# Graph message passing on one Trainium2 core: 20 chunks of edges move from gathering to counting, and the message add moves from VectorE to GpSimd

## The chip, the cores and the metric

The kernel runs on one core of one Trainium2 chip. A core has five engines that run their own instruction streams in order and meet through semaphores: TensorE (PE), VectorE (DVE), ScalarE (ACT), GpSimd (POOL) and SyncE (SP, which here only issues DMAs). The metric is the device time of one launch in microseconds. The kernel before was timed at 1654.11 us, the median of 3 runs (1650.71 to 1654.78).

## The reference

12,500 nodes have 64 features each; 400,000 edges, sorted by destination, have 64 features each. Most edges end at low node numbers, because the destination is drawn as 12,500 times the square of a uniform number.

```python
src = randint(400000, 0, 12500)
dst = (12500 * uniform(400000) ** 2).astype(int32)        # then both are sorted by dst
msg = node_feat[src] + edge_feat
agg = segment_sum(msg, dst, num_segments=12500)
h   = relu(agg @ W1 + b1)                                  # 64 -> 128
out = layernorm(x + h @ W2 + b2, axis=-1)                  # 128 -> 64, eps 1e-5
```

## The kernel before

**Chunks.** The edges are cut into 625 chunks of 640 (128 partitions by 5 columns). Every chunk has a *job*: SP loads the chunk's edge features, DVE compares the edges' destinations with 64 consecutive node numbers and writes a 0/1 matrix (`mark`, L809), PE multiplies five 128x64 blocks of features by it (`product`, L1026), and DVE adds the 64x64 result into the aggregate `agg` in SBUF (`add`, L831). Two jobs share a PSUM bank, and `add` runs two jobs behind `mark` (LAG = 2), so that DVE waits for both products of the pair.

**Two ways to get x[src].** The jobs above sum only edge features. The part with `x[src]` is brought in differently for the two kinds of chunk. For the last 205 chunks (the *gathered* ones, nodes of high number) POOL fetches the rows `x[src]` by indirect DMA, five instructions of 128 rows per chunk (`gather`, L550), into one of five slots of `xmsg`, and DVE adds them to the edge features before the product (`mix`, L803). For the first 420 chunks (the *counted* ones: CROWS = 84 rows of 5 chunks) nothing is gathered: the kernel counts how often each source node occurs for each destination node, and multiplies these counts by x.

**Counting.** Windows of 1 to 4 consecutive nodes get *passes* of 128 edges. Up to ten passes make a *slot*. For each slot DVE compares the low 7 bits of the sources (`oh_lo`, L847) and the high part together with the node (`oh_key`, L851) with row constants; PE multiplies the two (`count_slot`, L1042) and so counts in PSUM; ACT copies the counts of a unit of 3 to 5 nodes into `counts` (`keep_unit`, L652). About 128 nodes make a *block*, and for each block PE multiplies the counts of 98 groups of 128 source nodes by x, split into three bf16 parts (`multiply`, L1058: 98 matmuls per block, spread over the next block's slots). The sums are turned (L1070) and added to `agg`. Every 128 passes make a *group*, for which DVE searches the place of the edges in a table (L763, L768), POOL fetches the records (`load_records`, L559), DVE prepares keys (L776, L778), PE turns them (L1004, L1005) and ACT copies them (L628).

**What sets the order.** The order on every engine is written out ahead of time by slot number. `plan` makes units, slots and groups from the expected edge counts. `timeline` gives each slot a planned time between FIRST and LAST, by its cost, and deals out the gathers and the jobs: the gather number g stands before the slot whose planned time reaches 36 + chunk x g/5. All engines go through the slots 0, 1, 2, ... and put the jobs that belong to the slot ahead of its counting. Rings of three (`oh_lo`, `oh_key`, PSUM banks) keep DVE at most three slots ahead of PE. On SP, the load of a chunk into a slot of `gmsg` or `cmsg` waits for the product that used the slot before.

After the loop, 13 batches of nodes go through the two dense layers and the normalization (L1125 to L1139, L591).

Of the kernel before, what the change touches and what calls it, by code (L numbers as in the profile page):

```python
# [9 lines left out]
LN_EPS = 1e-5  # L10
PARTS = 3
TOP = 256
CROWS = 84
FINE = 16
RARE = 1e-7

# [81 lines left out]
def timeline(units, slots, groups, gathered, counted):  # L98

    cost = [x.n * (195 + 92 * x.width) + 500 for x in slots]  # L100
    S, total = len(slots), sum(cost)
    FIRST, LAST = 90.0, 36.0 + 6.8 * gathered + 1.4 * groups
    begin, run = [], 0
    for c in cost:
        begin.append(FIRST + (LAST - FIRST) * run / total)
        run += c
    chunk = (LAST - 36.0) / gathered
    gathers_at = [[] for _ in range(S + 1)]
    s = 0
    for g in range(5 * gathered):  # L110
        while s < S and begin[s] < 36.0 + chunk * g / 5:
            s += 1
        gathers_at[s].append(divmod(g, 5))
    jobs = [(36.0 + chunk * (k + 1) + 5.0, "gather", k) for k in range(gathered)]
    jobs += [(70.0 + (LAST - 70.0) * (i + .5) / counted, "count", i) for i in range(counted)]
    jobs.sort()
    jobs_at = [[] for _ in range(S + 1)]
    s = 0
    for place, (_, kind, i) in enumerate(jobs):
        t = jobs[min(place | 1, len(jobs) - 1)][0]  # L120
        while s < S and begin[s] < t:
            s += 1
        jobs_at[s].append((place, kind, i))
    return gathers_at, jobs_at


def build(nc, x, src, dst, edge_attr, w1, b1, w2, b2, out):
    f32, i32, i16, bf16 = mybir.dt.float32, mybir.dt.int32, mybir.dt.int16, mybir.dt.bfloat16
    f16 = mybir.dt.float16
    ALU, ACT, AX = mybir.AluOpType, mybir.ActivationFunctionType, mybir.AxisListType  # L130

    N, D = x.shape
    E = src.shape[0]
    HID = w1.shape[1]
    TILES = 5
# [4 lines left out]
    RT = TILES * TILES  # L140
    CCH = CROWS * TILES
    GCH = NCH - CCH
# [13 lines left out]
    LAST = N - (HI - 1) * P  # L156
# [3 lines left out]
    FINES = ROW // FINE  # L160
    CFINE = CROWS * FINES
    UNITS, SLOTS, WINDOWS, RANGES = plan(N, E, COUNTED, HI)
# [32 lines left out]
    for b in range(BLOCKS):  # L195
# [4 lines left out]
        to = min(s0 + n + 2, NS)  # L200
# [8 lines left out]
    OSLOTS = 4  # L209
    RING = 3  # L210
    TABLES = 3
    GSLOTS, XSLOTS, CSLOTS = 8, 5, 6

    edge_v = edge_attr.rearrange("(c p j) f -> c p (j f)", p=P, j=TILES)
    src_v = src.rearrange("(t e) -> t e", t=ROWS)
# [8 lines left out]
    with ExitStack() as ctx:  # L224
        def sb(name, shape, dt=f32):
            return ctx.enter_context(nc.sbuf_tensor(name, shape, dt))

        def sem(name):
            return ctx.enter_context(nc.semaphore(name))
# [18 lines left out]
        gmsg = sb("gmsg", [P, GSLOTS * TILES * D])  # L248
        xmsg = sb("xmsg", [P, XSLOTS * TILES * D])
# [38 lines left out]
        src_f, hi_i = stage[:, 0:ROW], stage[:, ROW:2 * ROW].bitcast(i32)  # L288
        record_out = counts[0][0:CROWS, 0:FINES * REC].bitcast(f32).rearrange("t (b k) -> t b k", k=REC // 2)
        pad_out = onehot[0][:, 0:5 * REC // 2]  # L290
# [56 lines left out]
        gin = [sem(f"gin{s}") for s in range(GSLOTS)]  # L347
        gathered = [sem(f"gathered{s}") for s in range(XSLOTS)]
        mixed = sem("mixed")
# [43 lines left out]
        for r, (b, w, j) in enumerate(WINDOWS):  # L393
            if j == 0:
                t = 1
# [10 lines left out]
        def _(sp):  # L406
# [32 lines left out]
            for i in range(CSLOTS):  # L439
                load_counted(i)  # L440

            sp.wait_ge(most_made, 1)
            sp.dma_start(most_dram.rearrange("(t k) -> t k", t=CROWS), most[0:CROWS, :]).then_inc(most_out, 16)
            sp.wait_ge(records_made, 2)
            sp.dma_start(record_dram[0:CFINE, :].rearrange("(t b) k -> t (b k)", t=CROWS),
                         counts[0][0:CROWS, 0:FINES * REC].bitcast(i16)).then_inc(records_out, 16)
            sp.wait_ge(most_out, 16)
# [64 lines left out]
        def _(pool):  # L512
# [32 lines left out]
            def gather(k, j):  # L545
                t = k % XSLOTS
                if k >= XSLOTS and j == 0:
                    pool.wait_ge(mixed, k - XSLOTS + 1)
                at, of = t * TILES + j, k * TILES + j
                pool.indirect_dma_start(xmsg[:, at * D:(at + 1) * D], None, x,  # L550
                                        bass.IndirectOffsetOnAxis(ap=idx_t[:, of:of + 1], axis=0)
                                        ).then_inc(gathered[t], 16)

            def load_records(g):
                pool.wait_ge(run_ready, g + 1)
                pool.wait_ge(records_out, 32)
                if g >= 2:
                    pool.wait_ge(tables_turned, g - 1)
                pool.indirect_dma_start(records[g % 2][:, :], None, record_dram,  # L559
                                        bass.IndirectOffsetOnAxis(ap=run_at[g % 2][:, 0:1], axis=0)  # L560
                                        ).then_inc(records_in[g % 2], 16)

            pool.wait_ge(taken["idx"], NTURNS["idx"])
            for s in range(NS + 1):
                for g in SEARCH.get(s - 3, []):
                    load_records(g)
                for k, j in GATHERS_AT[s]:
                    gather(k, j)
                    if (k, j) == (2, 4):
                        for g in range(EARLY_GROUPS):  # L570
                            load_records(g)

            pool.wait_ge(redo_known, 1)
            redo = pool.value_load(redo_i[0:1, 0:1], min_val=0, max_val=1)
# [145 lines left out]
        def _(dve):  # L720
# [74 lines left out]
            nc.vector.tensor_copy(node_ps, iota_row[:, :]).then_inc(iotas_set, 1)  # L795
            dve.wait_ge(iotas_set, 3)

            def mix(k):
                s, t = k % GSLOTS, k % XSLOTS
                dve.wait_ge(gin[s], 16 * (k // GSLOTS + 1))  # L800
                dve.wait_ge(gathered[t], 16 * TILES * (k // XSLOTS + 1))
                to = gmsg[:, s * TILES * D:(s + 1) * TILES * D]
                nc.vector.tensor_tensor(to, to, xmsg[:, t * TILES * D:(t + 1) * TILES * D], ALU.add).then_inc(mixed, 1)  # L803

            def mark(place, kind, i):
                c = i if kind == "count" else CCH + i
                if place >= OSLOTS:
# [54 lines left out]
            for s in range(NS + 1):  # L862
                for place, kind, i in JOBS_AT[s]:
                    mark(place, kind, i)
                    if kind == "gather":
                        mix(i)
                    if place >= LAG:
                        add(place - LAG)
                if s == NS:
                    for place in range(NCH - LAG, NCH):  # L870
                        add(place)
                for g in SEARCH.get(s, []):
                    search(g)
                for g in SUBTRACT.get(s, []):
                    subtract(g)
                for b in ADD_SUMS.get(s, []):
                    add_sums(b)
                if s in (3, 7):
                    k = s // 4
                    for h in range(2):  # L880
                        take_part(h, k)
                    dve.wait_ge(b2_parted, k + 1)
                    nc.vector.tensor_tensor(b2_sb[:, :], b2_sb[:, :], b2_parts[:, k, :], ALU.subtract).then_inc(b2_rest, 1)
                if s < NS:
                    make_slot(s)
# [20 lines left out]
            with dve.If(0 < redo):  # L906
# [5 lines left out]
                with dve.Fori(0, NCH) as c:  # L912
# [4 lines left out]
                    with dve.Fori(0, extra + 1) as w:  # L917
# [8 lines left out]
                        to = agg[:, bass.ds((first_at + w * WIN).with_bounds(min_val=0, max_val=N - 1), WIN)]  # L926
# [250 lines left out]
```

## Time and profile before

| | |
|---|---|
| median of 3 runs | 1654.11 us |
| the profiled execution | 1654.78 us, its span 1652.9 us |
| TensorE busy | 1415.9 us (86% of the span), granted clock 0.915 of full speed |
| VectorE busy | 1374.4 us (83%) |
| GpSimd busy | 1085.5 us (66%) |
| ScalarE busy | 841.5 us (51%) |
| gathers (L550) | 1025 instructions, 980 ns each |
| counting matmuls (L1042) | 4206 |
| matmuls of counts by x (L1058) | 4410, that is 45 blocks of 98 |

The profiled execution is one of the timed runs; the span goes from its first to its last instruction. Busy time is the union of an engine's instructions. The first 100 us are the set-up (sorting out the lists, the first gathers), the loop over the slots runs from about 101 to 1519 us, and the dense layers take the rest. In PE's and DVE's busy times by line, the end of an instruction overlaps the start of the next, so the lines of an engine add up to more than its union.

### The profile page before, as it was taken

How to read it: one execution, taken by the hardware profiler on the slowest of the kernel's cores; microseconds unless marked ns; L12 is line 12 of the kernel's file. 1: busy time of each engine (PE TensorE's matmuls, PEld its weight loads, DVE VectorE, ACT ScalarE, POOL GpSimd, SP SyncE). 2: the span in 40 equal slices, each digit the busy share in tenths (PEclk: the TensorE clock that was granted, in tenths of full speed). 3: DMA queues.
4: the chain of work that ended last, by engine and by line, in shares of the span. 5: the costliest groups of instructions: out<-in, count | busy, mean ns of one | idle time of the engine just before them, and what ended most of it. 6: DMA issues, size and time to landing. Idle time of an engine off the chain costs nothing.

```text
span 1652.9 us, 43132 instructions
## 1 busy us (share of the span) xinstructions
PE 1415.9 (86%) x15541; PEld 1181.1 (71%) x15542; DVE 1374.4 (83%) x3536; ACT 841.5 (51%) x1767; POOL 1085.5 (66%) x1138
## 2 busy tenths in 40 slices
PE   1155788888898988989999989999999999999996
PEld 1155666667787877867766668888888888888454
DVE  4479999989998998989989989888888888885233
ACT  1233446575355565554444445566566666664332
POOL 9677777777777776767667776666657676653011
PEclk8577889999999999999999999999999999999555
DMA  3733444444444443434443443333334333331122
GB/s 105 183 93 92 118 105 113 101 105 109 110 107 106 115 115 95 111 100 98 114 101 98 104 106 95 92 99 99 93 100 102 91 95 97 94 88 27 40 56 60
DMA packets 159195, 162.47 MB, mean 98 GB/s; under 512 B 53803, under 2 KB 141723, under 8 KB 158653
## 3 DMA queue, kind: packets, MB, share of 16 engines
q1 hardware_dynamic: 124603, 122.83, 26.2%
q0 software_dynamic: 34384, 36.90, 12.3%
q8 instruction: 126, 2.06, 0.5%
q14 instruction: 82, 0.67, 0.1%
HBM read 154.75 MB, written 4.85 MB: 97 GB/s over the span
## 4 chain that ended last, share of the span: by engine, by line
PE 46%; DVE 31%; issue 15%; DVEq 3%; POOL 2%; ACT 2%; DMA 1%; SPq 0%; POOLq 0%
PE sums_ps L1058 14%; DVE oh_key L851 13%; PE counted_ps L1042 12%; PE chunk_ps L1026 11%; DVE oh_lo L847 6%; DVE onehot L809 4%; PE counted_ps L1125 3%; PE chunk_ps L1139 3%; DVE lists L831 2%; POOL counts L520 2%; DVE gmsg L803 2%; PE turn_ps L1070 2%; DVE less_b L763 1%; DVEq L823 1%; PE chunk_ps L1135 1%
## 5 line engine op out<-in xcount | busy, mean ns | idle before, releaser
L550 POOL DMA_INDIRECT xmsg<-in_x,idx_t x1025 | 1004.5, 980 | 321.9 <-issue 309.4
L652 ACT CAST counts<-counted_ps 128x392 bf16<-128x392 f32 (+2 forms) x1375 | 675.2, 545 | 584.8 <-PE counted_ps L1042 570.6
L1042 PE MATMUL counted_ps<-oh_key,oh_lo 128*128 128x196 bf16 (+3 forms) x4206 | 513.2, 251 | 103.2 <-DVE oh_key L851 89.6
L851 DVE TENSOR_TENSOR oh_key<-counted_ps,tables 128x980 bf16<-128x980 f16 (+4 forms) x883 | 537.3, 608 | 0.0
L1058 PE MATMUL sums_ps<-x_parts,counts 128*128 128x193 bf16 (+4 forms) x4410 | 497.7, 250 | 0.0
L1058 PEld LDWEIGHTS sums_ps<-x_parts,counts 128*128 128x128 bf16 (+4 forms) x4410 | 399.0, 110 | 39.0 <-issue 2.1
L1042 PEld LDWEIGHTS counted_ps<-oh_key,oh_lo 128*128 128x128 bf16 x4206 | 289.9, 100 | 187.8 <-DVE oh_key L851 127.6
L847 DVE TENSOR_TENSOR oh_lo<-counted_ps,tables 128x640 bf16<-128x640 f16 (+3 forms) x883 | 406.0, 460 | 15.5 <-PE counted_ps L1042 14.1
L1026 PE MATMUL chunk_ps<-onehot,cmsg 128*64 128x64 f32 x4200 | 315.4, 228 | 12.0 <-DVE lists L831 12.0
L1026 PEld LDWEIGHTS chunk_ps<-onehot,cmsg 128*64 128x64 f32 x4200 | 277.0, 141 | 44.8 <-issue 37.5
L809 DVE TENSOR_TENSOR onehot<-counted_ps,rel_t 128x320 f32<-128x320 f32 x625 | 296.9, 475 | 0.4 <-issue 0.3
L831 DVE TENSOR_TENSOR lists<-lists,chunk_ps 64x64 f32 x625 | 128.4, 205 | 120.1 <-PE chunk_ps L1026 77.1
L1026 PE MATMUL chunk_ps<-onehot,gmsg 128*64 128x64 f32 x2050 | 166.6, 232 | 6.5 <-DVE gmsg L803 5.9
L1026 PEld LDWEIGHTS chunk_ps<-onehot,gmsg 128*64 128x64 f32 x2050 | 142.6, 144 | 24.6 <-DVE gmsg L803 12.1
L559 POOL DMA_INDIRECT records<-edge_records,run_at x33 | 31.3, 949 | 109.8 <-DVE run_at L768 106.2
L803 DVE TENSOR_TENSOR gmsg<-gmsg,xmsg 128x320 f32<-128x320 f32 x205 | 97.2, 474 | 0.0
L591 POOL TENSOR_TENSOR x_parts<-x_parts,rstd 128x512 f32<-128x512 f32 (+1 forms) x13 | 12.9, 993 | 127.2 <-DVE rstd L951 127.2
L937 DVE TENSOR_TENSOR x_parts<-chunk_ps,x_parts 128x512 f32<-128x512 f32 (+1 forms) x13 | 8.6, 661 | 72.8 <-PE chunk_ps L1139 71.6
L656 ACT ACTIVATE counted_ps<-counted_ps,less_top 128x392 f32<-128x392 f32 (+2 forms) x100 | 55.5, 555 | 3.2
L1139 PEld LDWEIGHTS chunk_ps<-w_sb,x_parts 128*128 128x128 f32 x196 | 42.8, 330 | 10.2 <-issue 10.2
L1125 PE MATMUL counted_ps<-lists,w_sb 64*128 (+2 forms) x50 | 46.2, 1079 | 1.8 <-issue 1.8
L1139 PE MATMUL chunk_ps<-w_sb,x_parts 128*128 128x64 f32 x196 | 45.2, 425 | 0.0
(94 smaller groups left out, 479.6 us busy)
## 6 DMA issues: line engine op xcount, KB each, us to landing
cmsg<-in_edge_attr SPq DMA_DIRECT2D x420, 160.0 KB
gmsg<-in_edge_attr SPq DMA_DIRECT2D x205, 160.0 KB
xmsg<-in_x,idx_t POOLq DMA_INDIRECT x1025
x_parts<-in_x SPq DMA_DIRECT2D x12, 256.0 KB, 3.3
out_nodes<-x_parts SPq DMA_DIRECT2D x12, 256.0 KB, 2.6
edge_records<-counts SPq DMA_DIRECT2D x1, 1575.0 KB
lists<-in_src SPq DMA_DIRECT2D x1, 1562.5 KB
lists<-in_dst SPq DMA_DIRECT2D x1, 1562.5 KB
```

The lines of the kernel that those rows point to most:

```text
L550: pool.indirect_dma_start(xmsg[:, at * D:(at + 1) * D], None, x, bass.IndirectOffsetOnAxis(ap=idx_t[:, of:of + 1], axis=0)).then_inc(gathe ...
L652: nc.scalar.copy(to, ps.rearrange("p (n h) -> p h n", h=HI)).then_inc(unit_kept, 1)
L803: nc.vector.tensor_tensor(to, to, xmsg[:, t * TILES * D:(t + 1) * TILES * D], ALU.add).then_inc(mixed, 1)
L809: nc.vector.tensor_tensor(onehot[place % OSLOTS][:, :].rearrange("p (j n) -> p j n", j=TILES), node_ps.unsqueeze(1).broadcast_to([P, TILES ...
L831: nc.vector.tensor_tensor(to, to, chunk_ps[place // 2 % 2][0:D, place % 2 * WIN:place % 2 * WIN + w], ALU.add).then_inc(added, 1)
L847: nc.vector.tensor_tensor(oh_lo[s % RING][:, 0:n * P].rearrange("p (k n o) -> p k n o", k=n, o=2), lo_ps.rearrange("p (n o) -> p n o", o=2 ...
L851: nc.vector.tensor_tensor(oh_key[s % RING][:, 0:n * w].rearrange("p (k n o) -> p k n o", k=n, o=2), key_ps[:, 0:w].rearrange("p (n o) -> p ...
L1026: mm = nc.tensor.matmul(chunk_ps[place // 2 % 2][0:D, place % 2 * WIN:place % 2 * WIN + w], rows_at[:, j * D:(j + 1) * D], onehot[place % ...
L1042: mm = nc.tensor.matmul(unit_ps[u % BANKS][:, col:col + slot.key_cols], oh_lo[s % RING][:, n * P:(n + 1) * P], oh_key[s % RING][:, n * slo ...
L1058: mm = nc.tensor.matmul(sums_ps[0:n, 0:XC], counts[b % 2][:, h * P:h * P + n], x_parts[:, h * XC:(h + 1) * XC], start=(h == 0), stop=(h == ...
L1125: mm = nc.tensor.matmul(count_ps[k][:, o:o + m], w1_sb[:, :], agg[:, bass.ds(within(b * FN + o, AGG - m), m)], start=True, stop=True)
L1139: mm = nc.tensor.matmul(chunk_ps[k][:, i * D:(i + 1) * D], hid[k][:, i * P:(i + 1) * P], w2_sb[:, :], start=False, stop=(i == n - 1), skip ...
```

## The change

CROWS goes from 84 to 88, so 440 chunks are counted and 185 gathered, where it was 420 and 205. By `plan` this gives 940 slots instead of 883, 4482 passes instead of 4206, 1513 units instead of 1375, 50 blocks instead of 45 and 36 groups instead of 33. The first 4206 passes are nearly the same; what is new is the counting for nodes 5716 to 6267 at the end.

`mix` moves from DVE to POOL, behind the second gather of the next chunk. `gmsg` gets ten slots instead of eight and `xmsg` three instead of five. The constants of `timeline` change: LAST becomes 36 + 7.4 x 185 + 1.4 x 36 (1455.4) where it was 36 + 6.8 x 205 + 1.4 x 33 (1476.2), and a gathered chunk's job stands 0.4 of a chunk and 1 us later after its gathers.

```diff
-CROWS = 84
+CROWS = 88
@@ timeline
-    FIRST, LAST = 90.0, 36.0 + 6.8 * gathered + 1.4 * groups
+    FIRST, LAST = 90.0, 36.0 + 7.4 * gathered + 1.4 * groups
...
-    jobs = [(36.0 + chunk * (k + 1) + 5.0, "gather", k) for k in range(gathered)]
+    jobs = [(36.0 + chunk * (k + 1.4) + 6.0, "gather", k) for k in range(gathered)]
@@ build
-    GSLOTS, XSLOTS, CSLOTS = 8, 5, 6
+    GSLOTS, XSLOTS, CSLOTS = 10, 3, 6
@@ gpsimd
+            def mix(k):
+                s, t = k % GSLOTS, k % XSLOTS
+                pool.wait_ge(gin[s], 16 * (k // GSLOTS + 1))
+                pool.wait_ge(gathered[t], 16 * TILES * (k // XSLOTS + 1))
+                to = gmsg[:, s * TILES * D:(s + 1) * TILES * D]
+                nc.gpsimd.tensor_tensor(to, to, xmsg[:, t * TILES * D:(t + 1) * TILES * D], ALU.add).then_inc(mixed, 1)
...
                 for k, j in GATHERS_AT[s]:
                     gather(k, j)
+                    if j == 1 and k:
+                        mix(k - 1)
...
+            mix(GCH - 1)
@@ vector
-            def mix(k):
-                s, t = k % GSLOTS, k % XSLOTS
-                dve.wait_ge(gin[s], 16 * (k // GSLOTS + 1))
-                dve.wait_ge(gathered[t], 16 * TILES * (k // XSLOTS + 1))
-                to = gmsg[:, s * TILES * D:(s + 1) * TILES * D]
-                nc.vector.tensor_tensor(to, to, xmsg[:, t * TILES * D:(t + 1) * TILES * D], ALU.add).then_inc(mixed, 1)
...
                 for place, kind, i in JOBS_AT[s]:
                     mark(place, kind, i)
-                    if kind == "gather":
-                        mix(i)
                     if place >= LAG:
                         add(place - LAG)
```

POOL, from its first gather on, before (`xmsg` are the gathered rows, `records` the fetched groups):

```order
L550 DMA xmsg<-in_x,idx_t 128x64 x15
L559 DMA records<-edge_records,run_at 128x384 x2
L550 DMA xmsg<-in_x,idx_t 128x64 x57
L559 DMA records<-edge_records,run_at 128x384
L550 DMA xmsg<-in_x,idx_t 128x64 x21
```

The same place after (L559 is now the line of `mix`, L566 that of the records):

```order
L550 DMA xmsg<-in_x,idx_t 128x64 x7
L559 TENSOR_TENSOR gmsg<-gmsg,xmsg 128x320
L550 DMA xmsg<-in_x,idx_t 128x64 x5
L559 TENSOR_TENSOR gmsg<-gmsg,xmsg 128x320
L550 DMA xmsg<-in_x,idx_t 128x64 x3
L566 DMA records<-edge_records,run_at 128x384 x2
L550 DMA xmsg<-in_x,idx_t 128x64 x2
L559 TENSOR_TENSOR gmsg<-gmsg,xmsg 128x320
```

After each five gathers POOL now carries one add of 128x320, with two gathers of the next chunk between a chunk's last gather and its add.

DVE in the late part of the loop before, a pair of jobs between two slots (`onehot` is `mark`, `lists` holds `agg`, the ISA rows set the address of the add):

```order
L851 TENSOR_TENSOR oh_key0<-counted_ps,tables0 128x980
L809 TENSOR_TENSOR onehot2<-counted_ps,rel_t 128x320
L803 TENSOR_TENSOR gmsg<-gmsg,xmsg 128x320
L831 ISA
L831 TENSOR_TENSOR lists<-lists,chunk_ps0 64x64
L809 TENSOR_TENSOR onehot3<-counted_ps,rel_t 128x320
L831 ISA
L831 TENSOR_TENSOR lists<-lists,chunk_ps0 64x64
L847 TENSOR_TENSOR oh_lo1<-counted_ps,tables0 128x640
```

And after, a like pair:

```order
L854 TENSOR_TENSOR oh_key0<-counted_ps,tables2 128x980
L812 TENSOR_TENSOR onehot2<-counted_ps,rel_t 128x320
L834 ISA
L834 TENSOR_TENSOR lists<-lists,chunk_ps0 64x64
L812 TENSOR_TENSOR onehot3<-counted_ps,rel_t 128x320
L834 ISA
L834 TENSOR_TENSOR lists<-lists,chunk_ps0 64x64
L850 TENSOR_TENSOR oh_lo1<-counted_ps,tables1 128x640
```

Only the add of `gmsg` and `xmsg` is gone from DVE; the rest stands as it did.

PE in the added slots at the end of the loop after (L1043 counts, L1059 multiplies counts by x, L1027 are the products of the jobs):

```order
L1043 MATMUL counted_ps<-oh_key0,oh_lo0 128x196 x5
L1059 MATMUL sums_ps<-x_parts,counts1 128x193 x10
L1043 MATMUL counted_ps<-oh_key1,oh_lo1 128x196 x5
L1059 MATMUL sums_ps<-x_parts,counts1 128x193 x10
L1027 MATMUL chunk_ps1<-onehot2,cmsg 64x64 x5
L1027 MATMUL chunk_ps1<-onehot3,gmsg 64x64 x5
```

A slot of five passes carries about nine or ten matmuls of counts by x, as in the last third of the loop before.

## Rows read from the trace of the kernel before

**Rows 1.** The page: busy time, then 40 slices and granted clock.
```profile
PE 1415.9 (86%) x15541; PEld 1181.1 (71%) x15542; DVE 1374.4 (83%) x3536; ACT 841.5 (51%) x1767; POOL 1085.5 (66%) x1138
...
PE   1155788888898988989999989999999999999996
...
DVE  4479999989998998989989989888888888885233
```

**Rows 2.** Busy by stretch: window, length, PE, PEld, DVE, ACT, POOL, clock, DMA, GB/s.
```profile
101.30:278.00 176.70, 124.88 (x1523) 106.10 (x1523) 167.94 (x380) 75.00 (x149) 137.38 (x130) 0.85 0.41 104
278.00:674.00 396.00, 350.22 (x4406) 304.02 (x4403) 369.94 (x924) 228.53 (x461) 292.22 (x303) 0.97 0.43 107
674.00:1049.20 375.20, 343.52 (x3634) 269.82 (x3634) 343.32 (x1045) 184.27 (x382) 260.18 (x271) 0.99 0.41 103
1049.20:1516.00 466.80, 451.89 (x5372) 407.22 (x5373) 403.74 (x1047) 288.49 (x703) 305.99 (x318) 0.99 0.36 92
```

**Rows 3.** Waits, 101.3 to 278 us: total, times, longest.
```profile
PE counted_ps L1042 <- DVE oh_key L851: 43.7, 39, 7.5
```

**Rows 4.** Waits from 1049.2 to 1516 us.
```profile
POOL records L559 <- DVE run_at L768: 65.7, 10, 9.8
DVE lists L831 <- PE chunk_ps L1026: 37.9, 36, 3.3
...
PE counted_ps L1042 <- DVE oh_key L851: 7.7, 8, 2.8
```

**Rows 5.** Timeline, DVE around one mix: start, duration, line.
```profile
178.43 0.20 DVE L831 TENSOR_TENSOR lists<-lists,chunk_ps 64x64 f32 x1
178.56 0.48 DVE L809 TENSOR_TENSOR onehot<-counted_ps,rel_t 128x320 f32<-128x320 f32 x1
178.96 0.47 DVE L803 TENSOR_TENSOR gmsg<-gmsg,xmsg 128x320 f32<-128x320 f32 x1
179.36 0.21 DVE L831 TENSOR_TENSOR lists<-lists,chunk_ps 64x64 f32 x1
```

**Rows 6.** PE by line, 1049.2 to 1516 us: L1042, then L1058, then L1026.
```profile
1049.20:1516.00 466.80, 161.58 (x1305) 0.99 0.36 92
...
1049.20:1516.00 466.80, 207.88 (x2027) 0.99 0.36 92
...
1049.20:1516.00 466.80, 131.25 (x1900) 0.99 0.36 92
```

**Rows 7.** Timeline, DVE, a slot without a job.
```profile
1304.94 0.48 DVE L847 TENSOR_TENSOR oh_lo<-counted_ps,tables 128x640 bf16<-128x640 f16 x1
...
1305.35 0.65 DVE L851 TENSOR_TENSOR oh_key<-counted_ps,tables 128x980 bf16<-128x980 f16 x1
...
1305.92 0.47 DVE L847 TENSOR_TENSOR oh_lo<-counted_ps,tables 128x640 bf16<-128x640 f16 x1
```

**Rows 8.** POOL's groups by shape: count, busy, mean ns, idle before.
```profile
L550 POOL DMA_INDIRECT xmsg<-in_x,idx_t x1025 | 1004.5, 980 | 321.9 <-issue 309.4 <-DVE gmsg L803 11.5 <-PE turn_ps L1005 0.6
...
L591 POOL TENSOR_TENSOR x_parts<-x_parts,rstd 128x512 f32<-128x512 f32 x12 | 12.5, 1043 | 127.2 <-DVE rstd L951 127.2
L520 POOL IOTA counts<- 1x1426 int16 x2 | 12.1, 6052 | 0.0
...
L591 POOL TENSOR_TENSOR x_parts<-x_parts,rstd 128x128 f32<-128x128 f32 x1 | 0.4, 401 | 0.0
```

**Rows 9.** Timeline, POOL and DVE: first gather, and one beside L860.
```profile
39.70 1.13 POOL L550 DMA_INDIRECT xmsg<-in_x,idx_t  x1 [0.16 <-issue]
...
104.56 0.95 POOL L550 DMA_INDIRECT xmsg<-in_x,idx_t  x1 [0.30 <-issue]
...
105.81 7.67 POOL L550 DMA_INDIRECT xmsg<-in_x,idx_t  x1 [0.30 <-issue]
105.92 6.74 DVE L860 TENSOR_TENSOR counts<-counts,x_parts 128x3136 f32<-128x3136 f32 x2
```

**Rows 10.** Timeline, POOL: the fifth gather of the chunk mixed at 178.96.
```profile
174.56 1.09 POOL L550 DMA_INDIRECT xmsg<-in_x,idx_t  x1 [0.30 <-issue]
```

## The prediction

> **What bounds the kernel now.** I read first the page's busy shares and slices. PE (86%) and DVE (83%) are both near the top, and their digits change places: DVE has the nines in the first half, PE in the second [rows 1]. An average can't decide here, so I cut the loop into four stretches [rows 2]. Their ends are the starts of the slots 88, 308, 616 and 882, found by counting the `oh_key` instructions, so that jobs and mixes can be counted for each. From 101 to 278 us DVE is busy 95% and PE 71%, and PE waits for `oh_key` [rows 3]: DVE bounds. From 278 to 674 it is DVE 93%, PE 88%; from 674 to 1049 both 91.5%. From 1049 to 1516 PE is busy 97% and DVE 86%; there DVE waits for PE's products (37.9 us) and PE hardly for DVE (7.7 us) [rows 4]. So PE bounds the last third, DVE the first eighth, and between them the two take turns, with 7 to 9% lost to their short rings. Last I looked at POOL, which takes the new work. Its gathers run back to back, and its idle time is a wait for DVE's search before the records, 65.7 us in the last third alone [rows 4]. It is ahead there and has room.
>
> **The parts of the change.** The order is fixed by slot number, so I cost the old slots and the added ones apart. All durations are from the profiled execution: 1654.8 us, a span of 1652.9 us and 1.9 us around it; the median is 0.7 us lower.
>
> *The mix leaves DVE.* By its record it lasts 0.47 us, but records overlap: it starts at 178.96 and the next instruction at 179.36, so it takes 0.40 us of DVE's time [rows 5]. The four stretches hold 25, 57, 54 and 62 mixes: 10.0, 22.8, 21.6 and 24.8 us.
>
> *Jobs are thinned out.* The same 625 jobs spread over 940 slots. By `timeline` the four stretches lose 4, 10, 12 and 12 jobs to the end and two go from slot 0, 40 in all. On DVE a job is a mark and an add, 0.40 and 0.13 us [rows 5]. On PE its ten records take 131.3/190 = 0.69 us; but PE's lines add up to more than the union (523 to 451.9 us in the last stretch, the small lines among them), so I count 0.863 of it, 0.60 us [rows 2, 6].
>
> *The old slots.* Now each stretch is as long as its longer engine allows. How full that engine gets I take from the stretches themselves: 95% for DVE a third ahead, 97% for PE 12% ahead, 91.5% where both are equal [rows 2].
> First: DVE 167.9 - 10.0 - 2.1 = 155.8, at 95% 164.0 us, 12.7 saved.
> Second: DVE 369.9 - 22.8 - 5.3 = 341.8; PE 350.2 - 6.0 = 344.2. They are equal now; at 92% that is 374 us, 22 saved, not the 28 by which DVE was relieved.
> Third: DVE 343.3 - 21.6 - 6.4 = 315.3; PE 343.5 - 7.2 = 336.3. PE is ahead by 6%; at 94.3%, between the two cases, 356.6 us, 18.6 saved.
> Fourth: DVE 403.7 - 24.8 - 6.4 = 372.5; PE 451.9 - 7.2 = 444.7, now 19% ahead; at 97.5% 456.1 us, 10.7 saved.
> Together 64 us. DVE is relieved of nearly 100 us, and the rest is covered by PE.
>
> *The added slots.* 57 slots, with 276 passes of the 196-column form, 490 matmuls for 5 blocks, the 40 jobs, 5 turns and 3 tables. On PE, each from the last stretch [rows 6]: 276 x 161.6/1305 = 34.2; 490 x 207.9/2027 = 50.3; 40 x 0.69 = 27.6; turns and tables some 6. The sum is 118, by 0.863 102, at 97.5% 104 us. A check: the last 267 slots before took 466.8 us, 1.75 us each, and 57 such are 100 us, in spite of slightly fewer products of counts in each. DVE needs 57 x 0.98 us [rows 7], 40 x 0.53 and a few us for three groups, 83 us, so it is not late; ACT copies 138 more units in the shade of both. Nothing hides these 104 us: they stand behind a PE that is already full.
>
> *POOL.* A gather takes 0.98 us and 0.30 us of issue in the mean; undisturbed, 0.94 and 0.30, 1.25 us from start to start [rows 8, 9]. 925 of them are 1156 us. The mix is not shown on POOL. The nearest row is the multiply of the last phase: 1043 ns for 512 columns, 401 for 128 [rows 8]; for 320 columns that gives 722 ns, and with the issue gap 1.02 us. From below it can't cost less than the 0.40 us of DVE; from above I take the 1.04 us of 512 columns, the gap, and a wait for the gathers to land. This wait is not shown either. A mix on DVE started 3.3 us after its fifth gather ended without having waited [rows 5, 10]; two gathers now cover about 2.5 us, so it is between nothing and 0.8 us. So a mix is 0.4 to 2.1 us; I take 1.02, the row. POOL then needs 1156 + 189 + 36 x 1.25 = 1390 us from 43 us on and would be done at 1433, over 100 us before the loop ends; that is the cover. It is thinnest early: by the order, POOL must have issued 322 gathers by slot 264, which is 43 + 402 + 66 + 10 = 521 us, where PE and DVE arrive at about 545. The wait for the records now stands ahead of mixes too; but the order puts a mix some 5 slots before its product, and POOL's wait ends as DVE's search does, before PE is there: nothing.
> The two engines can also block each other. The gather beside L860 took 7.67 us where its neighbours took 0.95, until DVE's add of two SBUF operands was done [rows 9]. If every add on POOL held DVE up like that, it would cost 185 x 0.72 = 133 us of DVE. Against it, gathers take their 0.95 us beside DVE's steady stream of adds and compares with one operand in PSUM, and those are nearly all of the loop: I take nothing, and put the other end under D.
> The Trainium skill has the rule between these two ends (SBUF — State Buffer, Who interferes with whom): the engines share a port pair as a lock, and an instruction of VectorE takes part in it when both its inputs are in SBUF or in a two-port mode. By the rule the loss is nothing but a few key copies; without it, up to 133 us of DVE.
> The Trainium skill speaks against the move (GPSIMD Engine Reference, 4.1 Engine selection): adds of two tensors belong on VectorE, GpSimd being some 2x slower. Row and rule agree, 0.72 against 0.40 to 0.47 us. By the rule the move loses where POOL bounds; by the rows POOL doesn't, and the sum is the same.
>
> *Start.* POOL's lists are 276 and 108 entries longer, in two copies; at 6052/1426 = 4.2 ns each [rows 8] that is 3.2 us, and the set-up waits for them; two more loads stand on SP, about 1 us. Two jobs and the mixes fewer in slot 0 give some 2 us back: +2 us. The bounds are 0 and 5 us.
>
> Sum: 1654.8 - 64 + 104 + 2 = 1696.8; less 0.7 for the median, 1696 us, 2.5% slower.
>
> **The rivals.**
> *A: DVE bounds the whole loop (faster).* For it: PE's busy is a model, and DVE has more nines early. If the loop went by DVE alone at its 90.8%, its work would go from 1284.9 us by -79 (mixes) -20 (jobs) +83 to 1269: (1269 - 1284.9)/0.908 = -17 us, with the start 1639 us. The place is the added slots: PE would have to take their 102 us into gaps. It decides by how full PE can be from 278 us on: its 1350 us of work less the first stretch's 122 are 1228; at 98% the kernel is as fast as before, and A needs 99.6%. Against it: from 1049 us on DVE waits for PE. 5%.
> *B: PE and DVE mesh better.* With slack on DVE the middle stretches fill as the last, all at 97.5%: 160 + 353 + 345 + 456 = 1314 for 1414.7, a gain of 101: 1660 us. For it: the losses there are waits of one for the other. Against: equal loads made these losses. 7%.
> *C: POOL becomes the bound.* It begins early when a mix with gap and wait is over about 1.4 us, and at the end when over 1.7. At 2.0 us POOL ends at 43 + 1156 + 45 + 370 = 1614, where the loop would have ended at some 1559: 1751 us. For it: the unknown landing and the small early slack. 10%.
> *D: the relief gives little.* Early gaps belong to the ring and stay; half the 64 us: 1728 us; none: 1760, and no less if POOL's adds block DVE. 8%.
> *My forecast* 70%, its own range 1675 to 1718.
>
> **How the numbers follow.** Changes within 0.3% (5 us) can't be told from none. Faster has A: 5%. The same has half of B: 4%. Slower has the rest, 91%. The range leaves out A and the far side of C and D: 1665 to 1735.
>
> **What would show it.** Loop end near 1560 us, not 1519. PE's busy total near 1500, at 97% in the last third; DVE's near 1355, at 91, 88 and 82% in the second to fourth stretch. L559 as TENSOR_TENSOR on POOL, 0.7 us, 185 times, with no wait above 1 us on the gathers; gathers at 0.95 us. Slot 616 at some 998 us where it was 1049. The forecast is wrong if PE waits for POOL's mix by over 20 us in total, if PE's records of the old slots get shorter, or if the first 883 slots take other than 1345 to 1360 us.

## The result: 3.2% slower, and the profile after

The changed kernel took 1706.98 us, the median of 3 runs (1704.24 to 1709.12), against 1654.11. The ratio is 1.0319 (95% interval 1.0302 to 1.0337). The forecast was 1696 us. The profiled span is 1703.1 us, 50.2 us more than before. The changed kernel ran twenty times in all, with a median of 1705.2 us; where an experiment differs from it by a few us only, I compare with that.

First the page of the kernel after: busy time, and PE and DVE in 40 slices.

```profile
PE 1472.2 (86%) x16343; PEld 1241.7 (73%) x16344; DVE 1356.6 (80%) x3465; ACT 901.4 (53%) x1918; POOL 1136.8 (67%) x1226
...
PE   1156788989899898999999899999999989999997
...
DVE  4469999999998888899899878887878877885233
```

PE gained 56 us and DVE lost 18 [rows 1]. DVE's nines are now rare after the first third. That alone doesn't say where the 50 us are, so I cut the loop at the same slots as before (0, 88, 308, 616, 882) and add the new slots and the end. The view gives window, length, then PE, PEld, DVE, ACT, POOL.

```profile
108.06:270.09 162.03, 117.41 (x1485) 99.31 (x1484) 155.51 (x347) 75.15 (x148) 128.31 (x125) 0.88 0.39 104
270.09:643.01 372.92, 335.68 (x4305) 293.82 (x4303) 342.90 (x847) 227.90 (x461) 287.77 (x308) 0.98 0.41 106
643.01:996.97 353.96, 327.70 (x3485) 263.90 (x3485) 316.44 (x967) 182.79 (x380) 255.42 (x275) 0.99 0.38 99
996.97:1462.33 465.36, 444.95 (x5266) 399.13 (x5265) 375.81 (x965) 288.03 (x702) 304.83 (x326) 0.99 0.34 90
1462.33:1558.95 96.62, 94.13 (x1121) 84.19 (x1119) 78.81 (x206) 62.86 (x154) 62.36 (x68) 1.00 0.28 69
1558.95:1703.00 144.05, 128.88 (x546) 81.85 (x544) 40.56 (x85) 39.78 (x58) 13.26 (x14) 0.60 0.20 45
```

Beside [rows 2] this is the whole account. The slots 0 and 882 of before stood at 101.3 and 1515.9 us.

| part | before | after | difference | forecast |
|---|---|---|---|---|
| set-up, until slot 0 | 101.3 | 108.1 | +6.8 | +2 |
| slots 0 to 88 | 176.8 | 162.0 | -14.8 | -12.7 |
| 88 to 308 | 395.9 | 372.9 | -23.0 | -22 |
| 308 to 616 | 375.3 | 354.0 | -21.3 | -18.6 |
| 616 to 882 | 466.7 | 465.4 | -1.3 | -10.7 |
| 57 new slots | - | 96.6 | +96.6 | } +104 |
| from the last slot to the end | 137.0 | 144.1 | +7.1 | } |

In the new slots PE is busy 97% and DVE 82%, and they are the loss. The +7.1 us of the end has a visible cause, in the timeline of PE after the last slot:

```profile
1560.95 8.55 PE L1059 MATMUL sums_ps<-x_parts,counts 128*128 128x193 bf16 x98
...
1573.46 8.55 PE L1059 MATMUL sums_ps<-x_parts,counts 128*24 128x193 bf16 x98
```

Before, one block of 98 matmuls stood alone at the end. Now there are two, since the 50th block has only 24 nodes and leaves the 49th hardly a slot to spread over; and a block of 24 nodes costs the 8.55 us of one of 128.

POOL kept up with its new work. First its add (shortest, median and longest in ns), its own waits for the gathers to land and the wait of PE's weight load for the add; then who waited for whom after, with total, times and longest:

```profile
L559 POOL TENSOR_TENSOR gmsg<-gmsg,xmsg x185: 856/872/887, 52.0 to 1558.5; 128x320 f32<-128x320 f32 x185
...
  DMA xmsg<-in_x,idx_t: 21.7, 21
...
  PEld chunk_ps L1027: 0.5, 3
```

```profile
POOL records L566 <- DVE run_at L778: 145.5, 24, 12.8
DVE lists L834 <- PE chunk_ps L1027: 124.7, 84, 10.4
...
DVE less_b L773 <- DMA most_b<-fine_most: 21.1, 1, 21.1
```

PE waited 0.5 us in all for POOL's adds, and POOL 21.7 us for gathers to land. POOL still waits for DVE's search, DVE waits more for PE's products than before (124.7 us to 77.1), and in the set-up DVE waits 21.1 us for the table, where it had been 11.4.

### The profile page after: what moved, and what is told of

Read it like the earlier page. It is cut to its first block, busy times and chain, and to the rows that moved or that the text cites. A ratio compares the mean times of both kernels' runs of the same rounds, so it can differ in the third digit from the quotient of the medians.

```text
span 1703.1 us, 45021 instructions
## 1 busy us (share of the span) xinstructions
PE 1472.2 (86%) x16343; PEld 1241.7 (73%) x16344; DVE 1356.6 (80%) x3465; ACT 901.4 (53%) x1918; POOL 1136.8 (67%) x1226
## 3 DMA queue, kind: packets, MB, share of 16 engines
q0 software_dynamic: 31328, 33.91, 10.6%
## 4 chain that ended last, share of the span: by engine, by line
PE 59%; DVE 20%; issue 12%; ACT 3%; POOL 2%; DVEq 2%; DMA 1%; SPq 1%; POOLq 0%
PE sums_ps L1059 19%; PE counted_ps L1043 16%; PE chunk_ps L1027 15%; DVE oh_key L854 8%; DVE oh_lo L850 5%; DVE onehot L812 3%; PE counted_ps L1126 3%; PE chunk_ps L1140 3%; POOL counts L520 2%; ACT counts L662 2%; PE turn_ps L1071 2%; DVE lists L834 2%; DVE less_b L773 1%; DVEq L826 1%; PE chunk_ps L1136 1%
## 5 line engine op out<-in xcount | busy, mean ns | idle before, releaser
L550 POOL DMA_INDIRECT xmsg<-in_x,idx_t x925 | 889.1, 961 | 257.3 <-issue 238.2
L662 ACT CAST counts<-counted_ps 128x392 bf16<-128x392 f32 (+2 forms) x1513 | 732.0, 540 | 566.8 <-PE counted_ps L1043 549.8
L1043 PE MATMUL counted_ps<-oh_key,oh_lo 128*128 128x196 bf16 (+3 forms) x4482 | 546.4, 250 | 98.6 <-DVE oh_key L854 80.3
L854 DVE TENSOR_TENSOR oh_key<-counted_ps,tables 128x980 bf16<-128x980 f16 (+4 forms) x940 | 570.6, 607 | 0.0
L1059 PE MATMUL sums_ps<-x_parts,counts 128*128 128x193 bf16 (+4 forms) x4900 | 545.6, 250 | 0.1
L1059 PEld LDWEIGHTS sums_ps<-x_parts,counts 128*128 128x128 bf16 (+4 forms) x4900 | 440.1, 107 | 39.4 <-issue 2.6
L850 DVE TENSOR_TENSOR oh_lo<-counted_ps,tables 128x640 bf16<-128x640 f16 (+5 forms) x940 | 430.1, 458 | 27.3 <-PE counted_ps L1043 25.1
L1043 PEld LDWEIGHTS counted_ps<-oh_key,oh_lo 128*128 128x128 bf16 x4482 | 315.1, 99 | 182.8 <-DVE oh_key L854 115.0
L1027 PE MATMUL chunk_ps<-onehot,cmsg 128*64 128x64 f32 x4400 | 326.0, 227 | 12.6 <-DVE lists L834 11.8
L1027 PEld LDWEIGHTS chunk_ps<-onehot,cmsg 128*64 128x64 f32 x4400 | 287.2, 141 | 46.0 <-issue 38.5
L834 DVE TENSOR_TENSOR lists<-lists,chunk_ps 64x64 f32 x625 | 126.1, 202 | 170.1 <-PE chunk_ps L1027 124.7
L559 POOL TENSOR_TENSOR gmsg<-gmsg,xmsg 128x320 f32<-128x320 f32 x185 | 161.5, 873 | 24.6 <-DMA xmsg<-in_x,idx_t 21.7
L1027 PE MATMUL chunk_ps<-onehot,gmsg 128*64 128x64 f32 x1850 | 147.5, 229 | 1.8 <-DVE lists L834 1.8
L1027 PEld LDWEIGHTS chunk_ps<-onehot,gmsg 128*64 128x64 f32 x1850 | 127.1, 143 | 16.1 <-issue 12.7
L566 POOL DMA_INDIRECT records<-edge_records,run_at x36 | 34.1, 946 | 150.9 <-DVE run_at L778 145.5
L773 DVE TENSOR_SCALAR_CACHE_REDUCE less_b<-most_b,node_t 128x777 bf16<-128x777 int16 (+33 forms) x36 | 32.0, 889 | 21.1 <-DMA most_b<-fine_most 21.1
```

The lines of the kernel that those rows point to most:

```text
L559: nc.gpsimd.tensor_tensor(to, to, xmsg[:, t * TILES * D:(t + 1) * TILES * D], ALU.add).then_inc(mixed, 1)
L662: nc.scalar.copy(to, ps.rearrange("p (n h) -> p h n", h=HI)).then_inc(unit_kept, 1)
L834: nc.vector.tensor_tensor(to, to, chunk_ps[place // 2 % 2][0:D, place % 2 * WIN:place % 2 * WIN + w], ALU.add).then_inc(added, 1)
L850: nc.vector.tensor_tensor(oh_lo[s % RING][:, 0:n * P].rearrange("p (k n o) -> p k n o", k=n, o=2), lo_ps.rearrange("p (n o) -> p n o", o=2 ...
L854: nc.vector.tensor_tensor(oh_key[s % RING][:, 0:n * w].rearrange("p (k n o) -> p k n o", k=n, o=2), key_ps[:, 0:w].rearrange("p (n o) -> p ...
L1027: mm = nc.tensor.matmul(chunk_ps[place // 2 % 2][0:D, place % 2 * WIN:place % 2 * WIN + w], rows_at[:, j * D:(j + 1) * D], onehot[place % ...
```

## Experiments

Every ratio is to the kernel before, on the same chip, with its 95% interval. Stretches are the slots' as above. My theory: the relief of DVE pays only where DVE bounds, and added slots stand behind PE. Its rivals are those of the prediction, above all A (DVE bounds throughout) and C (POOL becomes the bound).

### e1: CROWS = 88 alone

```diff
-CROWS = 84
+CROWS = 88
```

> The kernel before with CROWS = 88 and nothing else changed: the mix stays on VectorE (185 of them), eight and five slots, the old constants of the timeline. My theory (TensorE bounds the end of the loop, and the 57 added slots stand behind it in full): +104 us for the added slots and their end, +5 to +7 us in the set-up, about -20 us because 40 jobs and 32 mixes leave the first 883 slots; 1735 to 1755 us, ratio 1.05 to 1.06. Theory A (VectorE bounds throughout): its work rises by 83 - 20 - 8 = 55 us, 1715 us. A theory in which fewer gathers relieve the kernel: under 1690 us.

1740.05 us, ratio 1.0507 (1.0478 to 1.0536). The set-up is 8.4 us longer, the four stretches changed by -3.9, -0.8, -19.1 and +0.6 us, the new slots took 97.0 and the end 143. The 38 jobs and 31 mixes that left the old slots saved 23 us, nearly all in the third stretch, and the new slots cost as much as in the change, though the mixes are on DVE here. So more counting is the loss, and A's 1715 us is refuted.

### e2: the mix on VectorE, but one column

```diff
-                to = gmsg[:, s * TILES * D:(s + 1) * TILES * D]
-                nc.vector.tensor_tensor(to, to, xmsg[:, t * TILES * D:(t + 1) * TILES * D], ALU.add).then_inc(mixed, 1)
+                to = gmsg[:, s * TILES * D:s * TILES * D + 1]
+                nc.vector.tensor_tensor(to, to, xmsg[:, t * TILES * D:t * TILES * D + 1], ALU.add).then_inc(mixed, 1)
```

> The kernel before with the mix still on VectorE and all its semaphores, but adding one column of 320, so the output lacks most of x[src] for the gathered chunks. VectorE loses about 0.33 us for each of 205 mixes, 68 us, and GpSimd gets nothing. My theory (TensorE covers most of the relief): 40 to 50 us saved, some 10, 15, 15 and 5 us in the four stretches; 1605 to 1615 us. Theory A (VectorE bounds throughout): 68/0.908 = 75 us saved, 1580 us. Theory D (gaps belong to the ring): 20 us or less saved, over 1630 us.

1624.08 us, ratio 0.9827 (0.9810 to 0.9843): 30 us saved, less than the 40 to 50 I expected and far from the 75 of A. The stretches, in the same view:

```profile
101.50:273.10 171.60, 117.95 (x1520) 101.42 (x1519) 159.88 (x381) 75.29 (x149) 132.63 (x128) 0.87 0.42 107
...
1017.90:1483.20 465.30, 451.35 (x5372) 406.78 (x5373) 384.57 (x1047) 288.46 (x703) 300.00 (x318) 0.99 0.37 92
```

They saved 5.2, 14.7, 11.7 and 1.4 us. In the last one DVE lost 19 us of work and the stretch 1.4; PE is at 97% there as before. e1 and e2 together save 56 us in the old slots and the change 60, so its gain is about as large as the two reliefs together. By stretches they don't add up: e1 and e2 give 9.1, 15.5, 30.8 and 0.8 us, the change 14.8, 23.0, 21.3 and 1.3. That the totals are near is in part chance.

### e3: the added blocks hardly multiplied

```diff
-                for h in range(h0, h1):
+                for h in [h for h in range(h0, h1) if b < 45 or h in (0, HI - 1)]:
...
-            nc.vector.tensor_scalar(signs_row[:, 0:1], sums_ps[0:1, 256:257], float(COUNTED), None,
-                                    ALU.not_equal).then_inc(redo_step, 1)
+            nc.vector.tensor_scalar(signs_row[:, 0:1], sums_ps[0:1, 256:257], -1.0, None,
+                                    ALU.is_lt).then_inc(redo_step, 1)
```

> The changed kernel, in which the five added blocks (45 to 49) are multiplied by x for 2 of their 98 groups of sources only, and the test on the sum of counts always passes; their nodes' sums are wrong. 480 matmuls are gone from TensorE and nothing from the other engines. My theory (TensorE bounds the added slots): 480 x 0.0885 us = 42 us less, of which 17 in the two runs of 98 at the very end; 1660 to 1670 us. If VectorE bounds there: only the 17 us at the end, 1690 us.

1680.25 us, ratio 1.0165 (1.0141 to 1.0190), 27 us less than the change. It lies between the two forecasts, and the stretches say why:

```profile
1461.60:1549.20 87.60, 77.52 (x832) 58.77 (x830) 79.47 (x205) 61.23 (x154) 61.74 (x67) 0.98 0.31 75
```

The end got 16 us shorter, as expected. But the new slots went only from 96.6 to 87.6 us although PE lost about 17 us of work in them. PE is busy 88% and DVE 91% then, and PE's waits there are 4.8 us for ACT's copies, 2.5 us for DVE's keys and 1.5 us for `oh_key`; which of them holds the slots isn't shown. So PE bounds the new slots, but the next limit stands only 9 us behind; cheaper multiplies alone would not have saved the change.

### e4: the mix on GpSimd with the old split

```diff
-CROWS = 88
+CROWS = 84
```

> The changed kernel with CROWS = 84: the mix on GpSimd and all else of the change, but the old split into 420 counted and 205 gathered chunks. TensorE and VectorE alone would be done 60 us earlier than before, about 1595 us. GpSimd needs 1025 x 1.25 + 205 x (0.87 + 0.30) + 33 x 1.25 = 1562 us from 40 us on, with some 20 us of waits for landing, so it ends at some 1620 us, where the loop of before ended at 1519. My theory, that GpSimd's room is used up by 0.87 us adds and that this is what the fewer gathers pay for: 1730 to 1760 us. If GpSimd is not the bound: 1595 to 1600 us.

1711.56 us, ratio 1.0353 (1.0335 to 1.0370): POOL is the bound, though by less than I had worked out. Here is its stream, then the waits of this run:

```profile
803.03 0.94 POOL L550 DMA_INDIRECT xmsg<-in_x,idx_t  x1 [0.30 <-issue]
804.00 0.87 POOL L559 TENSOR_TENSOR gmsg<-gmsg,xmsg 128x320 f32<-128x320 f32 x1
805.03 0.96 POOL L550 DMA_INDIRECT xmsg<-in_x,idx_t  x1 [0.16 <-issue]
```

```profile
PE turn_ps L1005 <- DVE keys L788: 72.5, 22, 6.3
...
DVE lows L786 <- DMA records<-edge_records,run_at: 48.3, 18, 5.4
...
PE chunk_ps L1027 <- POOL gmsg L559: 24.6, 14, 6.6
```

One gather follows another at 1.25 us, and at 2.0 us with an add between: the add costs 0.75 us there. Its record says 0.87; it begins 0.03 us after the gather ends, and the gap before the next gather is 0.16 us instead of 0.30. POOL waits only 5.0 us for the search in the whole loop, so it is full, and its lateness arrives by two ways: PE waits 24.6 us for mixes, and DVE 48.3 us for the records, which stand behind adds and gathers on POOL; PE then waits for DVE's keys. So in the changed kernel the fewer gathers are what makes room for the adds. That POOL is the bound is read from these waits; no run took the adds out at CROWS = 84.

### e5: the stores of the set-up cut at row 80

```diff
+            for r0, r1 in ((0, 80), (80, CROWS)):
+                sp.dma_start(record_rows[r0:r1, :], counts[0][r0:r1, 0:FINES * REC].bitcast(i16)).then_inc(records_out, 16)
```

> The changed kernel, with the two stores of the set-up (the table of the largest destinations and the records) cut into rows 0 to 79 and rows 80 to 87. In it and in e1 the loop begins 7 to 8 us late, in e4 (84 rows) not, though e4 has ten slots too: so it hangs on the 88 rows, and the wait that grew is that for the table's load behind the records' store (11.4 to 21.1 us). Theory S (a store of 88 rows goes out over fewer DMA engines than one of 84, as the Trainium skill has it in DMA: Bandwidth and Descriptors, why a DMA increments its semaphore by 16): with 80 rows apart, 5 to 8 us back, slot 0 at 100 to 103 us, 1699 to 1702 us in all. Rival (5% more bytes, and lists that are 3 us later): nothing back, 1706 to 1708 us.

1700.85 us, ratio 1.0302 (1.0275 to 1.0330), 4 us under the median of the change's 20 runs. Slot 0 stands at 103.8 us instead of 108.1; in the other runs with 88 rows in one store (e1, e3, e8, e12) it stands at 107.1 to 110.4. The waits for the table, here and in e4 with its 84 rows:

```profile
DVE less_b L776 <- DMA most_b<-fine_most: 16.3, 1, 16.3
```

```profile
DVE less_b L773 <- DMA most_b<-fine_most: 12.1, 1, 12.1
```

So some 4 of the 6.8 us of set-up come from the form of a DMA, not from its bytes: 88 partitions in one store are slower than 80 and 8. It is about half of what the wait for the table grew by; with the stores cut at 80 it still goes up with the rows, 10.6 us at 82, 11.6 at 83, 14.6 at 86 and 16.3 at 88 (e6, e9, e7, e5). The Trainium skill has a rule that fits (DMA: Bandwidth & Descriptors, Why a DMA increments its semaphore by 16 and not by 1): a transfer is dealt to the largest number of engines up to 16 that divides its slowest dimension, which by the rule is 14 for 84 rows, 11 for 88 and 16 for 80. The trace agrees in direction; it doesn't show the engines one by one. e1, with eight slots, has the 88 rows' loss too (8.4 us), and e4, with ten, has none (slot 0 at 100.0 us), so the added loads are not the cause.

### e6, e9, e10, e11: fewer counted chunks, mix on VectorE

The kernel before with CROWS = 82 (e6) and 83 (e9), the stores cut as in e5; e10 and e11 are 83 and 82 with another pace:

```diff
-    begin, run = [], 0
-    for c in cost:
-        begin.append(FIRST + (LAST - FIRST) * run / total)
-        run += c
+    marks = ((0.0, 101.3), (0.1, 278.0), (0.349, 674.0), (0.698, 1049.2), (1.0, 1516.0))
+    begin = []
+    for k in range(S):
+        f = k / (S - 1)
+        (f0, t0), (f1, t1) = next((p, q) for p, q in zip(marks, marks[1:]) if f <= q[0])
+        begin.append(FIRST + (LAST - FIRST) * (t0 + (t1 - t0) * (f - f0) / (f1 - f0) - 101.3) / 1414.7)
```

> The kernel before with CROWS = 82 (856 slots, 43 blocks, 215 gathered chunks) and the stores cut at row 80. If added slots cost what e1 and the change showed (some 1.7 us each), 27 fewer give 46 us back: 1605 to 1612 us. GpSimd then needs 1075 x 1.28 + 40 + stalls, until some 1470 us, where the loop would end at 1472, so it may take part of it back: up to 1625 us. If the slots' cost came from somewhere else: 1650 us.

> The kernel before with CROWS = 83 (870 slots, 44 blocks, 210 gathered chunks), the stores cut at row 80, the mix on VectorE. In e6 (82) GpSimd had hardly any wait for the search left and the gain was 6 us of the 46 that 27 fewer slots are worth. Theory P (before stands near the balance of TensorE and GpSimd, and a slot less saves 1.7 us only as long as GpSimd has room): GpSimd needs 1050 x 1.30 + 33 x 1.25 + 64 until some 1470 us and has a little room, so 10 to 20 us are saved: 1633 to 1643 us. If GpSimd's early stretch, where it never waits, sets the pace already: 1645 to 1652 us.

> As e9, with the planned time of a slot taken from the trace of the kernel before (slots at 0, 10, 35, 70 and 100% of the list at 101, 278, 674, 1049 and 1516 us) in place of the cost formula, so that gathers and jobs are dealt out evenly in real time: 453 gathers by slot 308 where e9 has 467. If GpSimd's early stretch costs time in e9, this gives back up to 10 us: 1628 to 1638 us. If not, the same as e9.

> As e6, with the pace of e10. GpSimd is full from end to end: 1075 x 1.30 + 40 + 64 is 1500 us at the loop's end, which was 1504 in e6. So 3 to 10 us less than e6: 1636 to 1643 us, and no better than e10.

| kernel | time | ratio | slot 308 at | slot 792 at | last slot |
|---|---|---|---|---|---|
| before (84) | 1653 to 1655 | 1 | 674.0 | 1356.7 | 1515.9 |
| e9 (83) | 1630.76 | 0.9852 (0.9838 to 0.9867) | 683.8 | 1356.0 | 1493.9 |
| e6 (82) | 1646.18 | 0.9960 (0.9947 to 0.9974) | 700.8 | 1391.1 | 1503.6 |
| e10 (83, pace) | 1643.73 | 0.9934 (0.9920 to 0.9948) | 682.6 | 1366.9 | 1505.6 |
| e11 (82, pace) | 1658.02 | 1.0023 (1.0014 to 1.0032) | 698.6 | 1403.3 | 1518.6 |

e9 beats both kernels: a step of CROWS in the other direction, with the stores cut, gives 24 us, of which 1.2 us are a slot 0 that stands earlier. Thirteen slots less are worth 13 x 1.7 = 22 us, and it gets them, against a forecast of 10 to 20. e6 was a miss: of 46 us it kept 7. POOL's waits for the search fell from 106.2 us before to 59.6 in e9 and 36.4 in e6. Up to 670 us they were 13.6 us before, 2.4 in e9 and none in e6: POOL is full there, and slot 308 comes 10 and 27 us later than before.

```profile
POOL records L562 <- DVE run_at L771: 59.6, 17, 6.3
POOL xmsg L553 <- DVE gmsg L806: 15.6, 19, 10.2
```

```profile
PE turn_ps L1007 <- DVE keys L781: 34.0, 20, 6.1
PE chunk_ps L1029 <- DVE gmsg L806: 15.3, 17, 2.3
```

The first two lines are e9's, the others e6's, where the ready mixes and keys come late: PE waits 34.0 and 15.3 us for them, where it had been 23.9 and 5.9 before, as it did under POOL's bound in e4. That this is what took the 39 us is read from the waits and not tested by a run. My idea of an even pace (e10, e11) fell: 12 to 13 us slower than the same split by the cost formula, although it gave POOL its early room back (19.0 and 13.5 us of waits for the search up to 670 us). e10 against e9 was 5 us ahead at slot 88 (276.9 us to 282.1), 23 behind at slot 176 (426.9 to 404.3), level again from slot 308 to slot 616 (1053.1 to 1054.2), and lost 12 us after that. Why the formula's order is better in detail stays open.

### e7: CROWS = 86 with the mix on GpSimd

```diff
-CROWS = 88
+CROWS = 86
```

The stores are cut as in e5.

> The changed kernel with CROWS = 86 (911 slots, 47 blocks of which the last is full, 195 gathered chunks) and the stores cut at row 80. In e4 a mix costs GpSimd's stream 0.75 us (a gather after it starts 2.0 us after the one ahead, not 1.25). GpSimd needs 975 x 1.25 + 195 x 0.75 + 43 and some 40 of stalls, until 1490; TensorE and VectorE need the changed kernel's 1562 less 29 slots x 1.7, less 7 of set-up: 1506 us. With one burst of 98 at the end instead of two, -8 us: 1637 to 1650 us in all. If GpSimd is still the bound: 1665 us or more.

1686.51 us, ratio 1.0209 (1.0186 to 1.0232): it missed. It is 20 us better than the change. By the two spans, 19 us apart, the set-up gives 7 us, the 29 slots fewer 47 and the end, with one lone block instead of two, only 3; the old slots take 38 back. Slot 882 stands at 1493.1, 31 us behind the changed kernel's. POOL has no wait for the search over 2 us until 988 us, so it is full for 60% of the loop. My sum for POOL had counted its time to the end only; the end has slack, the first 900 us haven't.

### e8: the old constants of the timeline

```diff
-    FIRST, LAST = 90.0, 36.0 + 7.4 * gathered + 1.4 * groups
+    FIRST, LAST = 90.0, 36.0 + 6.8 * gathered + 1.4 * groups
...
-    jobs = [(36.0 + chunk * (k + 1.4) + 6.0, "gather", k) for k in range(gathered)]
+    jobs = [(36.0 + chunk * (k + 1) + 5.0, "gather", k) for k in range(gathered)]
```

> The changed kernel with the timeline's constants of before (6.8 and a job at (k + 1) chunks + 5). The jobs of gathered chunks stand 0.4 of a chunk, some 2 slots, earlier, their number per stretch is the same. My theory (only the amount of work in the slots counts): within 5 us of the change, 1702 to 1712 us. Rival (the later jobs disturb the last stretch, where TensorE was idle 5 us more than before, or save a wait for the mix): over 6 us away.

1713.90 us, ratio 1.0377 (1.0355 to 1.0399), 7 to 9 us slower than the change. So the new constants are a part of the change that pays by itself; the run sets LAST and the place of the jobs back together and doesn't say which of them it is. Slot 308 stands at 655.4 us instead of 643.0, 2.4 of it already at slot 0, and nearly half of it comes back. PE waits 4.5 us for the mixes instead of 0.5, which isn't enough to explain it. That only the amount of work counts was wrong by that much.

### e12: the add on GpSimd, but one column

```diff
-                to = gmsg[:, s * TILES * D:(s + 1) * TILES * D]
-                nc.gpsimd.tensor_tensor(to, to, xmsg[:, t * TILES * D:(t + 1) * TILES * D], ALU.add).then_inc(mixed, 1)
+                to = gmsg[:, s * TILES * D:s * TILES * D + 1]
+                nc.gpsimd.tensor_tensor(to, to, xmsg[:, t * TILES * D:t * TILES * D + 1], ALU.add).then_inc(mixed, 1)
```

> The changed kernel with its add on GpSimd cut to one column of 320; the output lacks most of x[src] for the gathered chunks. GpSimd's stream gets some 0.5 us shorter for each of 185 mixes, 90 us in all, and nothing else changes. Forecast's view (GpSimd isn't the bound of the changed kernel): at most 4 us less, 1702 to 1707 us. Rival C (GpSimd bounds its early part): its room before slot 308 was used up, so 10 to 25 us less, all of it won before slot 308.

1703.03 us, ratio 1.0298 (1.0282 to 1.0314), 4 us under the change, whose own interval overlaps it, and 2 us under the median of its 20 runs. The add fell from 872 to 201 ns, 124 us in all, and POOL's wait for the search rose by nearly as much:

```profile
POOL records L566 <- DVE run_at L778: 254.6, 31, 17.7
```

From 145.5 to 254.6 us: 109 of the 124 us that POOL was relieved of are waited away. Slot 308 stands at 640.8 instead of 643.0. The adds on POOL cost the changed kernel 0 to 4 us, and rival C is out for it.

## Why the prediction was right

It named the way, the range and the mechanism: most of what DVE is relieved of is covered by PE, and the added slots stand behind PE. The sum forecast +42 us and the span grew by 50. By its steps:

- *What bounds now.* Right. e2 relieved DVE alone, and the gain by stretch fell to 1.4 us in the last third.
- *The mix leaves DVE, jobs are thinned out, the old slots.* 64 us forecast, 60 measured, near in three stretches. Two of the three were luck in part, as PE's work was put too high there (below): in the second stretch PE was to be as long as DVE and is 7 us shorter, in the third PE has 327.7 us instead of 336.3, but fills only 92.6% of the stretch instead of 94.3%. The fourth was mis-sized: 10.7 forecast, 1.3 measured. I took away 7.2 us of PE's jobs and raised its filling to 97.5% since DVE had more slack. PE's busy time became 444.95 us, as forecast (444.7), but the filling fell to 95.6%. e1 has the same (447 of 467 us) with the mixes on DVE. The stretch takes 464.7 to 467.3 us in the kernel before, the change, e1 to e5, e8 and e12: neither 12 jobs fewer nor up to 28 us less work on DVE shortens it by more than some 2 us. What PE waits for there isn't one thing: the waits for `oh_key` and for ACT's copies grew from 14.2 to 19.2 us together. What sets this length stays open.
- *The added slots.* 104 us forecast, 96.6 + 7.1 measured. The place of the last 7 was not seen: the second lone block. PE bounds them, with the next limit 9 us behind (e3); DVE was "not late", but by little.
- *POOL.* No price in the change, as forecast (e12). In its parts: the record is 0.87 us, not 0.72, probably since the nearest row, a multiply, reads one operand that is a column per group of 64 (not tested); the stream pays 0.74 us (the median) to 0.85 (the mean) from gather to gather and not 1.02; and the landing cost 21.7 us of waits, hidden by POOL's slack. POOL's adds didn't hold DVE up: its `mark`, 475 ns in the mean before, takes 472. With 205 chunks (e4) POOL's work does decide, as rival C had it for a dearer mix.
- *Start.* Mis-sized: +2 forecast, +6.8 measured. The step costed entries of lists and queue places and overlooked that CROWS is also the number of partitions of a store (e5: 4.3 us).
- *The signs.* The loop's end (1559.0 us), slot 616 (997.0), the first 883 slots (1354.3 us), DVE's total and PE's wait for the mixes came as named. Besides the add's 0.87 us, three didn't. Six of POOL's 185 adds waited over 1 us for their gathers, up to 6.6. PE's total was to be near 1500 us and is 1472: the sum took PE's busy time for work that goes only with the jobs, 23 us off the old slots, and it fell by 45 (1270.5 to 1225.7). e2 shows the rest: no job is gone there, and PE's busy time in the same slots falls by 22 us, to 1248.7. In part PE's records themselves get shorter, most of all in the first stretch, which the prediction had named as a sign against it. These are the products (L1026) there, before and in e2, with the granted clock behind the count:

```profile
101.30:278.00 176.70, 62.49 (x766) 0.85 0.41 104
...
101.50:273.10 171.60, 57.74 (x762) 0.87 0.42 107
```

The mean goes from 82 to 76 ns while the granted clock goes from 0.85 to 0.87 of full speed. So where DVE bounds, PE's busy time isn't all work, and some of it goes when DVE gets faster. It didn't upset the mechanism, since DVE or the unfilled time set the length of these stretches.

| rival | what the runs say |
|---|---|
| A, DVE bounds throughout | refuted by the result, e1 and e2 |
| B, better meshing | no: the longer engine fills 92 and 93% of the second and third stretch, not 97.5% |
| C, POOL becomes the bound | not in the change (e12); by the waits, yes with CROWS 84 (e4) and early with 86 (e7) |
| D, the relief gives little | for the mix alone half true: 30 us of 68 (e2) |

## What to carry to other kernels

Cut the loop at the same step of the program in both kernels and read each engine's share in each stretch: work taken from an engine pays by the stretches in which it is ahead, here 30 us for some 68 (e2). Don't take the other engine's busy time there as fixed. Where a constant shifts work between two methods, test one step to either side before larger edits: here 83 instead of 84, with the stores cut, gave 1.5% and 88 cost 5.1% by itself. And look where else such a constant is used: this one was also the partition count of a DMA and the size of the last block.

## What was not expected of the hardware

- A store of 88 partitions delayed the load behind it more than 80 and 8 did, by 4.8 us (21.1 to 16.3 us of waiting), with the same bytes (e5).
- On POOL an add of 128x320 f32 with two SBUF operands is 872 ns and one of 128x1 is 201 ns, which is (872 - 201)/319 = 2.1 ns per column; between two gathers it adds 0.75 us where the gather pitch is 1.25.
- With the mixes gone from DVE, the mean gather fell from 980 to 961 ns. Beside the two long DVE adds of SBUF operands one gather each still takes 7 us (6.99 and 6.84), as in [rows 9]; in e4 it was an add on POOL that fell beside the second of them, and it took 7.04 us instead of 0.87.
